# A recommender kernel on one core: the last group of rows weighed slot by slot, a gate with its constant folded in, and matrix products that nobody reads

## The chip, the core and the metric

The kernel runs on one core of a Trainium2 chip. The metric is the device time of one execution in microseconds (us); lower is better. Of the kernel before there are three timed runs (median 819.96 us) and one profiled execution.

## What is computed

2048 users and items, 100 history entries for each user; D is 128, the two layers have 1024 and 512 features. Cut to what matters:

```python
hist_emb = user_table[history_users]                       # 2048 x 100 rows of 128
scores = jnp.einsum('bhd,bd->bh', hist_emb, user_emb)
user_his_emb = jnp.einsum('bh,bhd->bd', scores, hist_emb)
x = jnp.concatenate([items_emb, user_his_emb, user_emb], axis=1)
x = _dice(_batchnorm(x @ W1 + b1, g1, be1), a1)            # statistics over the 2048 users
x = _dice(_batchnorm(x @ W2 + b2, g2, be2), a2)
return x @ W3 + b3

def _dice(x, alpha):
    avg = x.mean(axis=1, keepdims=True)
    var = jnp.sum((x - avg) ** 2 + DICE_EPS, axis=1, keepdims=True)
    ps = jax.nn.sigmoid((x - avg) / jnp.sqrt(var))
    return ps * x + (1.0 - ps) * alpha * x
```

## The kernel before, in words

Indices past the table's end count as its last row, so most history entries are the same row; the kernel sorts each user's keys, ranks the users by how many entries are that last row, and treats them in 16 tiles of 128 users. It has three stages.

**Gathering (to about 607 us).** For each tile, GpSimd gathers the history rows that are not the last one, 128 rows (one slot) to an indirect DMA (L406). Four slots are a group, four groups the ring `rows` (16 slots). `relay` waits for each slot of a group to land; only the fourth raises `arrived` (L413), on which VectorE waits. VectorE's `weigh` (L623 to L642) multiplies a group by the user's row (L628), sums (L633), masks (L637) and, with `feed`, hands the indices of a later group to GpSimd (L642). ScalarE scales the four slots by their scores (L879) and TensorE adds them into `pooled_ps` by products with the identity (`add_rows`, L1052). A tile's last group g1 is weighed after the loop over its groups (L675). Ahead of it VectorE takes the statistics of the tile before (`layer1_stats`, L621, 8 `bn_stats`). After it, in the last tile alone, it aggregates 15 tiles' statistics (L680, 8 `bn_aggr`), and TensorE makes the last part of the first layer (`layer1_pooled`, L1039, 8 products).

**First batch norm and gate, second layer (about 612 to 768 us).** VectorE makes scale and shift of the 1024 features (L684 to L708; ready at `bn_ready`). The 2048 users then go through in 9 chunks: 0 and 1 of 128 users, 2 to 8 of 256. Each engine has its own order, written out by hand in a function `step(i, live)`, in which `live(n)` holds the work for chunk i - n. A chunk goes through these pieces:

- normalise: ScalarE (L915), and for some feature blocks GpSimd (L441) or, for chunk 0, VectorE (L712)
- the average over features: for chunks 0 and 1 (`c < NARROW`) eight TensorE products with a matrix of 1/1024 (L1111); for the others VectorE adds eight blocks to one (L765, L771, L781) and TensorE makes one product (L1116)
- the deviation (VectorE L733), its square (ScalarE L933), sums (VectorE L758, L768, L776), the variance (TensorE L1123), root (ScalarE L927) and reciprocal (VectorE L741), spread to all lanes (TensorE L1137), times the deviation (VectorE L749), sigmoid (ScalarE L939)
- the mix: gate * (1 - alpha) + alpha, by VectorE for chunks 0 and 1 (L720), by GpSimd for the others (L448), then times x (VectorE L725, `dice_done`)
- the second layer: 32 products (TensorE L1093), 8 of them ahead of the next chunk's L1137 and 24 behind it; ScalarE adds the bias (L948)

Every engine works in its order and waits on semaphores, so TensorE's average of chunk c stands in its queue ahead of the products of chunk c - 2.

**Second batch norm, gate and output (768 us to the end).** TensorE turns the result (L1148), VectorE takes statistics, and for each tile a gate and a weighted sum follow (L1153, L831); GpSimd scatters the outputs (L457).

```python
def relay(q, count):                                    # L409, GpSimd
    for j in range(GROUP):
        pool.wait_ge(landed[q * GROUP + j], count)
        pool.sem_inc(arrived if j == GROUP - 1 else passed, 1)
```

## Time and profile before

| | before |
|---|---|
| median of three runs | 819.96 us (819.0 to 820.18) |
| the profiled execution, its own time | 820.12 us |
| its span in the trace | 818.0 us |
| mean granted clock of TensorE, as a share of 2.4 GHz | 0.87 |
| busy: TensorE 78%, VectorE 63%, GpSimd 61%, ScalarE 43% of the span | |

The trace names the engines PE (TensorE), PEld (its weight loads), DVE (VectorE), ACT (ScalarE) and POOL (GpSimd). A busy TensorE isn't one at full speed: the granted clock is 1.00 or 0.50 at any one time, which is 2.4 or 1.2 GHz, and a share between them in a stretch is a mixture. A product of 32-bit numbers appears as two matmul records, so 64 records of L1093 are 32 products. Where an engine is idle before an instruction, the row tells in square brackets for how long, and what ended it.

### The profile page before, as it was taken

The numbers are of one execution on the slowest core, as the hardware profiler recorded it, in microseconds if no ns is written. First come the engines' busy times: TensorE is split into PE (matmuls) and PEld (weight loads), VectorE is DVE, ScalarE is ACT, GpSimd is POOL, SyncE is SP. The second block draws the span as 40 slices with busy tenths as digits, with TensorE's granted clock in tenths as the row PEclk, the third lists the DMA queues.
The fourth block names the chain that finished last, engine by engine and source line by source line (L and its number), as shares of the span: only waits on it lengthen the run. The fifth ranks groups of instructions, "written<-read, shape, count | busy, mean of one in ns | idle before, by whom it ended". The sixth has DMA issues, their size and how long they took to land.

```text
span 818.0 us, 16371 instructions
## 1 busy us (share of the span) xinstructions
PE 640.0 (78%) x3374; PEld 534.2 (65%) x3374; DVE 518.4 (63%) x1422; ACT 351.7 (43%) x858; POOL 496.7 (61%) x519
## 2 busy tenths in 40 slices
PE   0475759787887879878878898798654889999794
PEld 0473648565766757666766686586544878888684
DVE  7933446656665656666756666675556879985383
ACT  0002325343442534434444445345437777663452
POOL 7772777776777777777777777777742045321025
PEclk9967968796988978789898989889686789999998
DMA  7980221221111212122221222222210000000000
GB/s 147 54 154 26 52 53 51 55 52 52 52 54 51 56 53 53 51 56 53 52 56 52 53 56 53 54 54 53 52 34 0 1 1 0 1 1 1 0 2 0
DMA packets 19640, 35.73 MB, mean 44 GB/s; under 512 B 10552, under 2 KB 10752, under 8 KB 19584
## 3 DMA queue, kind: packets, MB, share of 16 engines
q0 software_dynamic: 15360, 30.45, 17.7%
q1 hardware_dynamic: 4224, 4.59, 1.9%
q8 instruction: 28, 0.46, 0.2%
q14 instruction: 28, 0.23, 0.1%
HBM read 35.00 MB, written 0.01 MB: 43 GB/s over the span
## 4 chain that ended last, share of the span: by engine, by line
issue 30%; PE 28%; POOL 16%; DMA 12%; DVE 6%; ACT 3%; DVEq 2%; POOLq 1%; ACTq 1%; SPq 0%; PEldq 0%
PE ps L1093 13%; POOL rows L406 11%; DMA rows<-in_L_rec_user_table_dram,slot_idx 11%; PE ps L993 5%; PE ps L1052 3%; PE ps L984 2%; POOL wide L387 2%; PE ps L1153 2%; POOL wide L402 2%; ACT wide L959 1%; PE ps L1148 1%; DMA wide<-in_L_rec_item_table_dram,ids 1%; DVE prod L628 1%; PE ps L1039 1%; ACTq L320 1%
## 5 line engine op out<-in xcount | busy, mean ns | idle before, releaser
L406 POOL DMA_INDIRECT rows<-in_L_rec_user_table_dram,slot_idx x432 | 407.6, 944 | 149.7 <-issue 112.3
L879 ACT ACTIVATE scaled<-rows,work 128x128 f32 (+1 forms) x492 | 175.7, 400 | 195.2 <-DVE work L637 114.4
L1052 PE MATMUL ps<-ident,scaled 128*128 128x128 f32 x984 | 174.7, 323 | 95.1 <-ACT scaled L879 94.3
L1052 PEld LDWEIGHTS ps<-ident,scaled 128*128 128x128 f32 x984 | 152.8, 221 | 121.2 <-issue 112.6
L628 DVE TENSOR_TENSOR prod<-rows,ps 128x512 f32<-128x512 f32 x123 | 84.2, 684 | 121.3 <-POOLq L413 79.1
L993 PE MATMUL ps<-wide,h 128*128 128x360 f32 x448 | 156.2, 507 | 0.0
L993 PEld LDWEIGHTS ps<-wide,h 128*128 128x128 f32 x448 | 92.1, 211 | 51.7 <-issue 13.4
L1093 PE MATMUL ps<-h,w 128*128 128x256 f32 (+1 forms) x576 | 119.1, 368 | 1.3 <-DVE h L725 1.3
L1093 PEld LDWEIGHTS ps<-h,w 128*128 128x128 f32 x576 | 102.9, 199 | 13.1 <-DVE h L725 1.6
L633 DVE TENSOR_REDUCE work<-prod 128x512 f32 x123 | 84.3, 686 | 14.3 <-DVE prod L628 5.5
L448 POOL TENSOR_SCALAR work<-work,rest,alphas 128x2048 f32<-128x2048 f32 x7 | 20.1, 2877 | 91.6 <-ACT work L939 91.6
L529 DVE SCALAR_TENSOR_TENSOR h<-ps,col_no 128x1024 f32<-128x1024 f32 x28 | 34.3, 1224 | 54.0 <-ACT ranked L851 52.5
L1033 PE MATMUL ps<-both_T,w 128*128 128x128 f32 x512 | 63.8, 279 | 0.0
L1033 PEld LDWEIGHTS ps<-both_T,w 128*128 128x128 f32 x512 | 61.1, 196 | 0.0
L851 ACT ACTIVATE ranked<-ps 128x360 f32<-128x360 f32 x15 | 7.1, 470 | 106.7 <-PE ps L993 97.3
L1039 PE MATMUL ps<-pooled_T,w 128*128 128x128 f32 x256 | 47.9, 366 | 0.5 <-ACT pooled_T L902 0.5
L1039 PEld LDWEIGHTS ps<-pooled_T,w 128*128 128x128 f32 x256 | 46.7, 281 | 0.8 <-ACT pooled_T L902 0.8
L457 POOL DMA_INDIRECT out_dram<-y_col,perm x16 | 15.4, 964 | 46.2 <-DVE y_col L824 43.5
L637 DVE SCALAR_TENSOR_TENSOR work<-wide,ends_f,work x123 | 27.4, 223 | 22.9 <-issue 13.6
L984 PE MATMUL ps<-wide,h 128*128 128x128 f32 (+2 forms) x128 | 29.4, 416 | 15.3 <-DVE h L523 12.0
L984 PEld LDWEIGHTS ps<-wide,h 128*128 128x128 f32 x128 | 25.2, 281 | 19.1 <-DVE h L523 12.3
L871 ACT ACTIVATE h<-ps,par 128x128 f32<-128x128 f32 x128 | 35.9, 361 | 1.8 <-DVE stats L684 1.6
(173 smaller groups left out, 684.9 us busy)
## 6 DMA issues: line engine op xcount, KB each, us to landing
rows<-in_L_rec_user_table_dram,slot_idx POOLq DMA_INDIRECT x432, 2.5
w<-in_L_rec_W_dram SPq DMA_DIRECT2D x1, 2048.0 KB, 9.6
w<-in_L_rec_W_dram SPq DMA_DIRECT2D x1, 1536.0 KB, 9.6
h<-in_r_history_users_dram SPq DMA_DIRECT2D x1, 800.0 KB, 5.2
wide<-in_L_rec_user_table_dram,ids POOLq DMA_INDIRECT x16, 7.0
wide<-in_L_rec_item_table_dram,ids POOLq DMA_INDIRECT x16, 6.9
out_dram<-y_col,perm POOLq DMA_INDIRECT x16, 2.1
last_row<-in_L_rec_user_table_dram SPq DMA_DIRECT2D x1, 64.0 KB, 4.9
```

What stands on the lines that cost most here:

```text
L406: nc.gpsimd.indirect_dma_start(rows[:, s, :], None, user_table, bass.IndirectOffsetOnAxis(slot_idx[:, s:s + 1], 0)).then_inc(landed[s], 16)
L529: nc.vector.scalar_tensor_tensor(places[:, :, j, :], rank.rearrange("p (m j) -> p m j", j=2)[:, :, j].unsqueeze(2).to_broadcast(shape), -f ...
L628: nc.vector.tensor_tensor(prod[:, :, :], rows[:, at, :], user_now.unsqueeze(1).to_broadcast([P, GROUP, D]), ALU.mult).then_inc(multiplied, 1)
L633: nc.vector.tensor_reduce(raw[:, pair], prod[:, :, :], AX_X, ALU.add).then_inc(dotted, 1)
L871: nc.scalar.activation(h1[:, m, t * P:(t + 1) * P], l1_ps[:, m, :], ACT.Identity, bias=b1c[:, m:m + 1]).then_inc(l1_kept, 1)
L879: nc.scalar.activation(scaled[:, j, :], rows[:, bass.ds((g & (GROUPS - 1)) * GROUP + j, 1), :], ACT.Copy, scale=score[:, bass.ds(g * GROUP ...
L984: mm = nc.tensor.matmul(place_ps, at_place[:, t, :], people[:, t, x], start=(t == 0), stop=(t == TILES - 1))
L993: mm = nc.tensor.matmul(rows_ps[(t + 1) % 2], places[:, m, j, :], people[:, 2 * m + j, :], start=(j == 0 and m == 0), stop=(j == 1 and m = ...
L1033: nc.tensor.matmul(l1_ps[:, m, :], w1[:, k, m * P:(m + 1) * P], both_T[:, of:of + P], start=(k == 0 and m == blocks.start), stop=False, sk ...
L1039: mm = nc.tensor.matmul(l1_ps[:, m, :], w1[:, 1, m * P:(m + 1) * P], pooled_T[:, :], start=False, stop=True, skip_group_check=True)
L1052: nc.tensor.matmul(pooled_ps, scaled[:, j, :], ident[:, :], start=False, stop=False, skip_group_check=True).then_inc(slot_summed, 1)
L1093: mm = nc.tensor.matmul(l2_ps[c % 2][:, o, 0:w], w2[:, k, o * P:(o + 1) * P], h1[:, k, chunk(c)], start=(k == 0), stop=(k == M1 - 1))
```

## The change

- `relay` raises `arrived` for each slot; `weigh` waits for `g * 4 + 4`. The last group of the last tile is weighed by a new `weigh_end`, slot by slot, and ScalarE scales each slot on its own score (`end_scored`).
- In the last tile the loop over groups is split after four of them; between the two parts stand `layer1_stats` of the tile before and the 8 `bn_aggr`, which stood ahead of and behind the last group.
- The mix is gone on both engines. The gate adds alpha / (1 - alpha) (`over`) in the multiplication by x, and the factor 1 - alpha (`rest`) is the scale of the second layer's bias step on ScalarE.
- `DIRECT = 4`: chunks 0 to 3 have their averages by eight TensorE products; VectorE's adding begins with chunk 4.
- `keep_busy` issues products of the identity with itself into a bank that is written anew before anything reads it: 8 ahead of the last group's `add_rows`, 12 after the last `layer1_pooled`, 5 after chunk 0's variance and 10 after chunk 0's L1137.

```diff
@@ relay (GpSimd)
-                    pool.sem_inc(arrived if j == GROUP - 1 else passed, 1)
+                    pool.sem_inc(arrived, 1)
@@ step (GpSimd)
-                if live(2) and i - 2 >= NARROW:
-                    c = i - 2
-                    pool.wait_ge(gated, c + 1)
-                    nc.gpsimd.tensor_scalar(dev_of(c), dev_of(c), rest[:, 0:1], alphas[:, 0:1],
-                                            ALU.mult, ALU.add).then_inc(mixed, 1)
                 if live(-1):
                     normalise(i + 1)
@@ weigh and weigh_end (VectorE)
-                hold(dve, arrived, g + 1)
+                hold(dve, arrived, g * GROUP + GROUP)
...
+            def weigh_end(g, t, bound):
+
+                for j in range(GROUP):
+                    hold(dve, arrived, g * GROUP + (j + 1))
+                    one = bass.ds(g * GROUP + (t * GROUP + j), 1)
+                    nc.vector.tensor_tensor(prod[:, j:j + 1, :], rows[:, bass.ds((g & (GROUPS - 1)) * GROUP + j, 1), :],
+                                            user_now.unsqueeze(1), ALU.mult).then_inc(end_multiplied, 1)
+                    dve.wait_ge(end_multiplied, j + 1)
+                    nc.vector.tensor_reduce(raw[:, one], prod[:, j:j + 1, :], AX_X, ALU.add).then_inc(end_dotted, 1)
+                    dve.wait_ge(end_dotted, j + 1)
+                    nc.vector.scalar_tensor_tensor(score[:, one], slot_no[:, bass.ds(g * GROUP + j, 1)], bound, raw[:, one],
+                                                   ALU.is_lt, ALU.mult).then_inc(end_scored, 1)
@@ the loop over tiles (VectorE)
-                with dve.Fori(0, g1 - g0) as r:
+                with dve.Fori(0, g1 - g0 if t + 1 < TILES else GROUPS) as r:
...
+                if t + 1 == TILES:
+
+                    layer1_stats(t - 1)
+                    dve.wait_ge(stats_done, M1 * t)
+                    for m in range(M1):
+                        nc.vector.bn_aggr(mv[:, m, :], stats1[:, m, 0:t, :].rearrange("p t s -> p (t s)")).then_inc(bn_step[0], 1)
+                    with dve.Fori(GROUPS, g1 - g0) as r:
+                        g = dve.snap(r + g0).with_bounds(max_val=HIST * (t + 1) // GROUP - 1)
+                        weigh(g, t, ALU.is_ge, ends_f[:, t:t + 1], True)
...
-                if t:
+                if t and t + 1 < TILES:
                     layer1_stats(t - 1)
-                weigh(g1, t, ALU.is_lt, ends_f[:, t + 1:t + 2])
-
-
-            dve.wait_ge(stats_done, M1 * (TILES - 1))
-            for m in range(M1):
-                nc.vector.bn_aggr(mv[:, m, :], stats1[:, m, 0:TILES - 1, :].rearrange("p t s -> p (t s)")).then_inc(bn_step[0], 1)
+                if t < TILES - 1:
+                    weigh(g1, t, ALU.is_lt, ends_f[:, t + 1:t + 2])
+                else:
+                    weigh_end(g1, t, ends_f[:, t + 1:t + 2])
@@ step (VectorE)
-                    if c < NARROW:
-                        dve.wait_ge(gated, c + 1)
-                        nc.vector.tensor_scalar(dev_of(c), dev_of(c), rest[:, 0:1], alphas[:, 0:1],
-                                                ALU.mult, ALU.add).then_inc(mixed_first, 1)
-                        dve.wait_ge(mixed_first, c + 1)
-                    else:
-                        dve.wait_ge(mixed, c - NARROW + 1)
-                    nc.vector.tensor_tensor(h1[:, :, chunk(c)], by_block(dev_of(c), M1), h1[:, :, chunk(c)],
-                                            ALU.mult).then_inc(dice_done, 1)
+                    dve.wait_ge(gated, c + 1)
...
+                    nc.vector.scalar_tensor_tensor(h1[:, :, chunk(c)], by_block(dev_of(c), M1), over[:, 0:1], h1[:, :, chunk(c)],
+                                                   ALU.add, ALU.mult).then_inc(dice_done, 1)
...
-                if live(0) and i >= NARROW:
+                if live(0) and i >= DIRECT:
@@ scale_rows and step (ScalarE)
+                by_slot = t == TILES - 1 and after is end_scaled
+                if not by_slot:
+                    hold(act, scored, g + (t + 1))
                 for j in range(GROUP):
+                    if by_slot:
+                        act.wait_ge(end_scored, j + 1)
...
                         nc.scalar.activation(h2[:, k, chunk(c)], l2_ps[c % 2][:, k, 0:w], ACT.Identity,
-                                             bias=b2c[:, k:k + 1]).then_inc(l2_kept, 1)
+                                             bias=b2c[:, k:k + 1], scale=rest[:, 0:1]).then_inc(l2_kept, 1)
@@ TensorE
+            def keep_busy(count):
+
+                for _ in range(count):
+                    nc.tensor.matmul(idle_ps, ident[:, :], ident[:, :], start=True, stop=True)
...
+                if t == TILES - 1:
+                    keep_busy(8)
                 add_rows(g1, t, True)
...
             layer1_pooled(TILES - 1)
+            keep_busy(12)
...
-                    if c < NARROW:
+                    if c < DIRECT:
```

TensorE's order from the end of the first layer to the first products of the second, before (`mean_of` is the matrix of 1/1024, `h` the features, `w` the weights):

```order
L1039 MATMUL ps<-pooled_T,w 128x128 x8
L1111 MATMUL ps<-h,mean_of 128x128 x16
L1123 MATMUL ps<-ones,sq_sum 128x1
L1137 MATMUL ps<-ident,inv 128x128
L1116 MATMUL ps<-col_sum,mean_of 128x256
L1123 MATMUL ps<-ones,sq_sum 128x1
L1093 MATMUL ps<-h,w 128x128 x8
```

and with the change:

```order
L1066 MATMUL ps<-pooled_T,w 128x128 x8
L1049 MATMUL ps<-ident 128x128 x12
L1141 MATMUL ps<-h,mean_of 128x128 x16
L1153 MATMUL ps<-ones,sq_sum 128x1
L1049 MATMUL ps<-ident 128x128 x5
L1169 MATMUL ps<-ident,inv 128x128
L1049 MATMUL ps<-ident 128x128 x10
L1141 MATMUL ps<-h,mean_of 128x256 x8
L1153 MATMUL ps<-ones,sq_sum 128x1
L1123 MATMUL ps<-h,w 128x128 x8
```

The unread products are the rows `ps<-ident`; chunk 2's average, one product of 256 columns, is eight and still stands ahead of chunk 1's variance and of the products of chunk 0.

VectorE's order from chunk 0's L749 to its multiplication by x, before:

```order
L749 TENSOR_TENSOR work<-work,ps 128x1024
L758 TENSOR_TENSOR rows<-rows 128x512
L765 TENSOR_TENSOR w<-h 128x1024
L768 TENSOR_TENSOR rows<-rows 128x256
L771 TENSOR_TENSOR w<-w 128x512
L776 TENSOR_TENSOR sq_sum<-rows 128x128
L781 TENSOR_TENSOR col_sum<-w 128x256
L720 TENSOR_SCALAR work<-work,rest,alphas 128x1024
L725 TENSOR_TENSOR h<-work,h 128x8x128
L733 TENSOR_TENSOR work<-h,ps 128x2048
```

and with the change (`over` is alpha / (1 - alpha)):

```order
L767 TENSOR_TENSOR work<-work,ps 128x1024
L776 TENSOR_TENSOR rows<-rows 128x512
L786 TENSOR_TENSOR rows<-rows 128x256
L794 TENSOR_TENSOR sq_sum<-rows 128x128
L743 SCALAR_TENSOR_TENSOR h<-work,over,h 128x8x128
L751 TENSOR_TENSOR work<-h,ps 128x2048
```

Four instructions are gone from between the two: three of chunk 2's adding and the mix; the multiplication is one instruction with three inputs.

VectorE's order in the last tile, from the end of the loop over groups to the aggregation, before:

```order
L667 COMPARE_AND_BRANCH
L621 BN_STATS stats<-h 128x6 x8
L313 ISA
L628 REGISTER_ALU
L628 ISA
L628 TENSOR_TENSOR prod<-rows,ps 128x512
L313 REGISTER_ALU
L633 ISA
L633 TENSOR_REDUCE work<-prod 128x4
L637 ISA
L637 SCALAR_TENSOR_TENSOR work<-wide,ends_f,work 128x4
L680 BN_AGGR mv<-stats 128x2 x8
```

and with the change, from the end of the loop's first part:

```order
L679 COMPARE_AND_BRANCH
L620 BN_STATS stats<-h 128x6 x8
L688 BN_AGGR mv<-stats 128x2 x8
L689 UNCONDITIONAL_BRANCH
L689 ISA
L627 REGISTER_ALU
L627 ISA
L627 TENSOR_TENSOR prod<-rows,ps 128x512
```

Both statistics now stand ahead of the loop's second part, in which (at L627) a whole group is still weighed; the last group's slots follow after that. On GpSimd the 16 normalisations, which stood in pairs behind the mixes from the ninth on, follow each other, with nothing to wait for after the scale and shift.

## Rows read from the trace of the kernel before

**Rows 1.** The page: busy time, share of the span and instructions by engine.

```profile
PE 640.0 (78%) x3374; PEld 534.2 (65%) x3374; DVE 518.4 (63%) x1422; ACT 351.7 (43%) x858; POOL 496.7 (61%) x519
```

**Rows 2.** By stretches: length, busy of PE, PEld, DVE, ACT, POOL; granted clock; DMA.

```profile
606.90:612.30 5.40, 2.05 (x8) 1.78 (x8) 4.85 (x11) 1.48 (x5) 0.00 (x0) 0.65 0.00 0
620.00:624.10 4.10, 3.89 (x18) 3.92 (x19) 1.12 (x6) 3.15 (x9) 3.96 (x8) 0.50 0.00 0
630.60:637.00 6.40, 1.44 (x5) 1.21 (x5) 6.37 (x10) 6.29 (x9) 0.00 (x0) 0.50 0.00 0
657.10:662.10 5.00, 1.85 (x7) 1.62 (x7) 5.00 (x5) 4.39 (x10) 5.00 (x2) 0.76 0.00 0
662.10:668.20 6.10, 6.10 (x20) 5.05 (x21) 2.20 (x2) 3.20 (x3) 0.73 (x2) 0.64 0.00 1
668.20:768.30 100.10, 99.67 (x483) 87.99 (x481) 73.01 (x80) 53.15 (x75) 27.83 (x12) 1.00 0.00 1
```

**Rows 3.** GpSimd's four releases of the last group (one line's instructions, 601.5 to 607).

```profile
L413 POOLq EVENT_SEMAPHORE  x4: 17/17/17, 601.9 to 606.5; - x4
```

**Rows 4.** The timeline, last tile: start us, us, engine, line [idle before].

```profile
595.86 0.69 DVE L628 TENSOR_TENSOR prod<-rows,ps 128x512 f32<-128x512 f32 x1 [1.19 <-POOLq L413]
...
600.87 0.69 DVE L628 TENSOR_TENSOR prod<-rows,ps 128x512 f32<-128x512 f32 x1 [2.75 <-POOLq L413]
...
603.69 1.65 DVE L621 BATCH_NORM_STATS2 stats<-h 128x6 f32<-128x128 f32 x8 [0.57 <-issue]
...
606.88 0.69 DVE L628 TENSOR_TENSOR prod<-rows,ps 128x512 f32<-128x512 f32 x1 [1.54 <-POOLq L413]
...
608.80 0.22 DVE L637 SCALAR_TENSOR_TENSOR work<-wide,ends_f,work  x1 [0.29 <-DVE work L633]
...
608.94 3.49 DVE L680 BATCH_NORM_AGGREGATE mv<-stats 128x2 f32<-128x90 f32 x8
...
612.60 3.35 PE L1039 MATMUL ps<-pooled_T,w 128*128 128x128 f32 x16 [0.46 <-ACT pooled_T L902]
```

**Rows 5.** The timeline from the first scale and shift to the first product of L1093.

```profile
619.65 4.32 POOL L441 TENSOR_SCALAR h<-h,scale,shift 128x128 f32<-128x128 f32 x8 [15.67 <-DVE shift L708]
...
619.65 1.37 DVE L712 TENSOR_SCALAR h<-h,scale,shift 128x128 f32<-128x128 f32 x5
...
620.21 6.37 PE L1111 MATMUL ps<-h,mean_of 128*128 128x128 f32 x32 [4.26 <-ACT h L915]
...
624.00 1.22 DVE L733 TENSOR_TENSOR work<-h,ps 128x1024 f32<-128x1024 f32 x1 [2.98 <-PE ps L1111]
...
629.66 0.80 PE L1137 MATMUL ps<-ident,inv 128*128 128x128 f32 x2 [1.40 <-DVE inv L741]
...
630.50 1.22 DVE L749 TENSOR_TENSOR work<-work,ps 128x1024 f32<-128x1024 f32 x1 [0.89 <-PE ps L1137]
...
632.24 1.22 DVE L765 TENSOR_TENSOR w<-h 128x1024 f32<-128x1024 f32 x1
...
634.85 0.80 DVE L720 TENSOR_SCALAR work<-work,rest,alphas 128x1024 f32<-128x1024 f32 x1
...
635.68 1.23 DVE L725 TENSOR_TENSOR h<-work,h 128x1024 f32<-128x1024 f32 x1
...
636.97 3.79 PE L1093 MATMUL ps<-h,w 128*128 128x128 f32 x16 [0.48 <-DVE h L725]
```

**Rows 6.** The timeline of chunk 2, from its L749 to its products.

```profile
651.50 5.52 PE L1093 MATMUL ps<-h,w 128*128 128x128 f32 x48
...
651.70 2.29 DVE L749 TENSOR_TENSOR work<-work,ps 128x2048 f32<-128x2048 f32 x1 [0.87 <-PE ps L1137]
...
656.09 3.13 POOL L448 TENSOR_SCALAR work<-work,rest,alphas 128x2048 f32<-128x2048 f32 x1 [32.13 <-ACT work L939]
...
657.38 2.11 DVE L776 TENSOR_TENSOR sq_sum<-rows 128x256 f32<-128x256 f32 x1
...
659.75 2.28 DVE L725 TENSOR_TENSOR h<-work,h 128x2048 f32<-128x2048 f32 x1
...
662.08 5.91 PE L1093 MATMUL ps<-h,w 128*128 128x256 f32 x16 [0.28 <-DVE h L725]
...
668.28 10.53 PE L1093 MATMUL ps<-h,w 128*128 128x256 f32 x48
```

**Rows 7.** Groups of instructions by form: count, busy us, mean ns, idle before.

```profile
L529 DVE SCALAR_TENSOR_TENSOR h<-ps,col_no 128x1024 f32<-128x1024 f32 x28 | 34.3, 1224 | 54.0 <-ACT ranked L851 52.5 <-issue 0.2
...
L653 DVE COPY ps<-ranked 128x128 f32<-128x128 f32 x16 | 4.7, 295 | 9.2 <-DVE work L637 9.2
```

46 lines of the change are left out of this document (27 added, 19 removed).

## The prediction

> **What bounds the kernel now.** I read the page first. TensorE is the busiest engine at 78% [rows 1], but a share of the whole span hides three stages with three limits, so I went on to the busy times by stretches, and then to the timeline around the places that the diff touches. Up to 607 us the gathers on GpSimd set the pace. From 668.20 to 768.30 TensorE is busy for 99.67 of 100.10 us at clock 1.00 [rows 2]: there nothing helps but fewer products. The last 50 us (818.0 - 768.3) aren't touched by the diff, except for where two constants are kept. What is left is the stretch of 61 us between 607 and 668, in which TensorE waits for others, falls to half its clock and then works at half: the granted clock is 0.65 in 606.90:612.30, 0.50 in 620.00:624.10, 0.50 in 630.60:637.00, and 0.64 in 662.10:668.20, where it is busy all the time [rows 2]. A gain can come from there alone, and it counts only as far as chunk 2's products (L1093 at 662.08 [rows 6]) start earlier or run faster, since from there on TensorE has no gap.
>
> **The last group and the statistics.** Two edits meet here. The statistics were 8 `bn_stats` of 1.65 us and 8 `bn_aggr` of 3.49 us [rows 4]. The `bn_aggr` cost nothing where they were: they ended at 612.43 (608.94 + 3.49), and L1039, on which VectorE's next work depends, began only at 612.60 [rows 4]. So moving them gains nothing by itself; it is needed only if the last group gets shorter. The last tile has five groups in its loop, the fourth at 595.86 and the fifth at 600.87 [rows 4]; the new place is behind the fourth. A group takes 2.26 us (600.87 to its end at 603.12, which is where the idle 0.57 us before L621 began). So the fourth ends at 598.12, and behind it come 0.57 us of loop end, 5.14 us of statistics and some 0.3 us of loop start: the fifth group starts at 604.1 in place of 600.87 and ends at 606.4. The slots of the last group are released from 601.9 to 606.5 [rows 3], so when VectorE comes to them at about 607.1 all four are there, and going slot by slot no longer hides any of their landing. It now costs: a slot is three instructions, two of about 0.29 us (128x128, the copy L653 [rows 7]) and one of 0.22 (L637 [rows 4]), with some 0.15 us between dependent ones (0.26 to 0.29 before, where two register waits stand between), about 1.15 us in all. The fourth score is there at 607.1 + 4 x 1.15 = 611.7, where all four were at 609.02 (L637 [rows 4]). In return ScalarE and TensorE have one slot left to do, not four: from the score to L1039 it was 3.58 us (612.60 - 609.02), and is about 1.8. L1039 starts at 613.5, so **0.9 us later**. Of TensorE: the fifth group's additions end at 608.9, then come the 8 unread products, at half clock 8 x 0.42 = 3.4 us (L1039 has 8 in 3.35 us [rows 4]), so until 612.3; the slots' additions go behind them, and are just not held up. TensorE is then busy from 607.5 on without a long gap. L1111 tells how its clock comes back: 16 products in 6.37 us [rows 5], where all at half would be 6.7 and all at full 3.8, and 0.50 until 624.10 [rows 2]; so it rose some 5 us after the work began. L1039 should then run at the full clock: 8 x 0.24 = 1.9 us in place of 3.35 (24 products of 128 columns take 5.52 us, L1093 at 651.50 [rows 6]), **1.4 us less**. Together the scale and shift come 0.3 us earlier, since VectorE's own statistics of the last tile then pace it. Ends: 1.2 us later (no full clock), 1.8 us earlier (VectorE needs 0.95 us a slot and less for the loop's ends).
>
> **The first two averages.** The 12 unread products take 2.9 us at full clock in a gap of 4.26 us (idle before L1111 [rows 5]). If they keep the clock up, chunk 0's average ends 1.2 us after VectorE's last normalisation (L712 ends at 621.0 [rows 5], then 620.7; the rest of it are the last products and the way to VectorE), and L733, at 624.00 [rows 5], comes at about 622.4, allowing 0.5 us for ScalarE's share. **1.6 us earlier**, the 0.3 from above in it. From here to L749 the chain is one of dependent steps that don't change, ScalarE's normalisation of chunk 2 among them: L749 at 628.8 for 630.50.
>
> **Chunk 0's gate and its products.** Behind L749 VectorE loses four instructions: L765, L771 and L781, of 1024, 512 and 256 columns, and the mix L720. From L765 to L725 it was 3.44 us (632.24 to 635.68 [rows 5]), in which only two small sums stay, 0.7 us together by their size against L765's 1.22 for 1024 columns; 2.7 us go. The multiplication stays as long: with three inputs 128x1024 takes 1224 ns at L529 [rows 7], with two 1.23 us at L725 [rows 5]. So L725 could start at 631.3 for 635.68. But TensorE isn't ready. Ahead of the products it has 10 unread ones (2.4 us) and chunk 2's average, which was one product and is eight of 0.44 us (24 in 10.53 us, L1093 [rows 6]), 3.5 us. L1137 began at 629.66 and took 0.80 us at half clock [rows 5]; 1.7 us earlier and at full it ends at 628.5, and 628.5 + 2.4 + 3.5 and 0.1 for a variance gives 634.5, or **2.5 us earlier** than 636.97 [rows 5], and the 10 unread products are a part of what holds it up.
>
> **Chunk 2, where it counts.** From 634.5 at full clock: 32 products of 0.24 us with L1137 between them, and a wait of 0.7 us for it, until about 643.0, then chunk 3's average in 3.6 us, until 646.6; chunk 3's deviation starts at 646.8 and chunk 2's L749 at 649.9, for 651.70 [rows 6]: **1.8 us earlier**. Of the 2.5 us and of the half clock in chunk 0's products most goes into two averages that are each 7 x 0.44 = 3.1 us longer. From L749 to L725 it was 8.05 us (651.70 to 659.75 [rows 6]). There the mix of GpSimd shows: L776 takes 2.11 us for 256 columns, while L448 runs beside it [rows 6]; without it 256 columns should take 0.4 (512 take 0.69, L628 [rows 4]). The mix is gone, so **1.6 us** go too. L725 starts at 656.3, chunk 2's products at 658.7. Then the clock: before, 0.64 over 6.10 us is 4.4 us at half, which cost 2.2 us. TensorE's idle time ahead was 3.1 us (it worked 1.85 of 5.00 in 657.10:662.10 [rows 2]) and is about the same now, so it may fall or not; I take half, **1.0 us**.
>
> **GpSimd's normalisations** take 0.54 us each (8 in 4.32 us, L441 [rows 5]); 16 now run in one go, from 619.3 to 628. In the trace nothing on VectorE that reads two tiles of SBUF stood beside the first eight. The Trainium skill (SBUF — State Buffer, Who interferes with whom) says that a VectorE instruction with two SBUF inputs and a GpSimd instruction that reads SBUF exclude each other, whole instruction by whole instruction; L776 beside L448 agrees, with 2.11 us. By that rule L758, L768 and L776 of chunk 0, at 625 to 627, can each wait 0.54 us, up to 1.6 us, and the sum below would be 817.2. From the rows alone the bounds are 0 (L441 beside L712 showed no delay) and 3 x 0.54 = 1.6; I take 0, as TensorE, not this chain, holds up chunk 0's products, and keep 1.6 for the range.
>
> **Other edits** are worth nothing: one register instruction more in VectorE's wait for a group lies under gathers that VectorE waits for (idle 2.75 and 1.54 us before L628 [rows 4]), and the scale 1 - alpha is in an instruction that is there anyway.
>
> **The sum.** 1.8 (of which 0.3 and 1.3 come from the first two parts) + 1.6 + 1.0 = 4.4 us. The profiled execution had 820.12 us, 2.1 over its span and 0.16 over the median; 819.96 - 4.4 = 815.6 us. A measurement of this kernel tells 0.2%, 1.6 us, from no change.
>
> **The rivals.**
> - *The clock holds.* The clock stays full from the last group to the end: then chunk 2's 2.2 us come back whole, and with the last group at its better end (1.5 us) the time is 815.6 - 1.2 - 1.5 = 812.9. The Trainium skill (TensorE: Matmul & The Clock Gate, What's actually happening) says that the half clock is the default and activity lifts it; for it speaks 668 to 768 at 1.00, against it that a gap of 3 us stays ahead of chunk 2. Chance 0.20.
> - *Late and in the way.* VectorE's chain is later by the last group (1.2) and by the normalisations (1.6), and this passes on to chunk 2; what stays is 4.4 - 2.8 = 1.6, and without the 1.0 of the clock 0.6: 819.4. Chance 0.12.
> - *Unread products at half clock.* They do not lift the clock, and stand in TensorE's order. The last group and L1039: 1.2 us later. The 12 take 5.0 us in a gap of 4.26: 0.8. The 5 take 2.1 us where at most 1.4 us were idle (before L1137 [rows 5]): 0.7. Then 10 take 4.2 us, and chunk 2's average at half 7.0: chunk 0's products start at 630.46 + 2.7 + 4.2 + 7.1 = 644.5, 7.5 us late. From there TensorE is no longer waiting, and what it lost before (1.9 us at half clock in the first eight of chunk 0's products, 3.79 for 1.9 [rows 5], half as much in the rest, 3.1 idle, 2.2 in chunk 2's) is 8.1 us, against 3.1 for chunk 3's average: 7.5 + 3.1 - 8.1 = 2.5 us slower, 822.5. It decides if the granted clock is still 0.50 while chunk 2's average runs. For it: 0.50 over all of 630.60:637.00 [rows 2] and little real work there; against: at 620.21 the clock did rise under products of the same size. Chance 0.08.
>
> **How the numbers follow.** The forecast has 0.60, from 813 to 818.3 by its own bounds (the last group 1.5 to either side, the clock 1.1, the normalisations 1.6). Its slower edge reaches into no change only a little. Faster by over 0.2%: 0.60 + 0.20 = 0.80. Within: 0.12. Slower: 0.08. The range is 811.8 to 819.2 us, which leaves out the third rival, some of the second and the far end of the first.
>
> **What would show it.** Right: the fifth group's L628 near 604 and the last score near 611.7; L1039's eight products in 2 us, not 3.35; L733 of chunk 0 at 622.4, its products at 634.5 at clock 1.00; sums of squares for chunk 2 in 0.4 us; chunk 2's products at 658.7; the stretch from there to the end as before. Wrong: a granted clock of 0.50 under the unread products before chunk 2's average, a chunk 0 whose L758 to L776 are stretched, or products of chunk 2 that start no earlier than 661.

## The result and the profile after

| | before | after |
|---|---|---|
| median of the runs | 820.05 us (8 runs, 819.0 to 820.97) | 812.27 us (8 runs, 809.95 to 816.31) |
| ratio, 95% interval | | 0.9908, 0.9889 to 0.9926 |
| profiled execution, its span | 820.12, 818.0 us | 812.3, 810.5 us |
| granted clock of TensorE, mean | 0.87 | 0.889 |

The kernel became 7.8 us faster where 4.4 were forecast. That is inside the range, 0.5 us from its faster end, and next to the rival "the clock holds" (812.9). The page of the changed kernel, busy times, against [rows 1]: GpSimd lost seven instructions and 30 us, VectorE 11 us, and neither number says where the gain is.

```profile
PE 637.8 (79%) x3472; PEld 533.6 (66%) x3472; DVE 507.3 (63%) x1423; ACT 355.3 (44%) x858; POOL 466.9 (58%) x512
```

The changed kernel by stretches (the columns are those of [rows 2]):

```profile
606.50:611.83 5.33, 4.87 (x28) 4.63 (x28) 2.24 (x9) 1.92 (x6) 0.00 (x0) 0.68 0.01 3
617.60:621.70 4.10, 3.54 (x29) 3.46 (x30) 2.59 (x6) 3.49 (x9) 4.10 (x8) 1.00 0.00 0
626.50:632.30 5.80, 5.80 (x40) 5.39 (x38) 3.83 (x5) 5.77 (x9) 0.32 (x1) 1.00 0.01 3
651.14:656.14 5.00, 2.57 (x21) 2.28 (x20) 5.00 (x7) 4.98 (x12) 0.00 (x0) 1.00 0.00 0
656.14:662.34 6.20, 6.20 (x31) 5.53 (x32) 4.21 (x3) 4.62 (x4) 0.00 (x0) 1.00 0.00 1
662.34:759.73 97.39, 97.39 (x471) 85.94 (x469) 64.54 (x80) 55.50 (x73) 0.00 (x0) 1.00 0.00 1
```

The three places that were at 0.50, 0.50 and 0.64 are at 1.00: the first average, the wait for chunk 0's gate, chunk 2's products. The long stretch is as full as before.

The last tile of the changed kernel, from the timeline (fifth group, slots, unread products, first layer's end; answers to [rows 4]):

```profile
597.26 1.65 DVE L620 BATCH_NORM_STATS2 stats<-h 128x6 f32<-128x128 f32 x8
598.94 3.50 DVE L688 BATCH_NORM_AGGREGATE mv<-stats 128x2 f32<-128x90 f32 x8
602.36 0.63 DVE L627 TENSOR_TENSOR prod<-rows,ps 128x512 f32<-128x512 f32 x1
...
605.11 0.29 DVE L648 TENSOR_TENSOR prod<-rows,ps 128x128 f32<-128x128 f32 x1 [0.59 <-issue]
...
606.35 0.29 DVE L648 TENSOR_TENSOR prod<-rows,ps 128x128 f32<-128x128 f32 x1
...
607.15 3.33 PE L1049 MATMUL ps<-ident 128*128 128x128 f32 x16
...
609.74 0.22 DVE L653 SCALAR_TENSOR_TENSOR work<-wide,ends_f,work  x1 [0.18 <-DVE work L651]
...
611.83 2.05 PE L1066 MATMUL ps<-pooled_T,w 128*128 128x128 f32 x16 [0.46 <-ACT pooled_T L924]
```

The slots come 1.24 us apart, the last score is there at 609.96, and the first layer's last products take 2.05 us for 3.35. From the first scale and shift to chunk 2's products (answers to [rows 5] and [rows 6]):

```profile
617.59 9.23 POOL L445 TENSOR_SCALAR h<-h,scale,shift 128x128 f32<-128x128 f32 x16 [14.62 <-DVE shift L729]
...
618.15 4.07 PE L1141 MATMUL ps<-h,mean_of 128*128 128x128 f32 x32 [1.59 <-ACT h L937]
620.48 1.22 DVE L751 TENSOR_TENSOR work<-h,ps 128x1024 f32<-128x1024 f32 x1 [1.51 <-PE ps L1141]
...
622.69 3.04 ACT L937 ACTIVATE h<-h,shift,scale 128x256 f32<-128x256 f32 x6
...
623.56 0.66 DVE L786 TENSOR_TENSOR rows<-rows 128x256 f32<-128x256 f32 x1
624.25 0.53 DVE L794 TENSOR_TENSOR sq_sum<-rows 128x128 f32<-128x128 f32 x1
...
625.64 0.24 ACT L949 ACTIVATE root<-ps,var_eps 128x1 f32<-128x1 f32 x1
...
628.74 3.62 PE L1141 MATMUL ps<-h,mean_of 128*128 128x256 f32 x16
629.47 1.28 DVE L743 SCALAR_TENSOR_TENSOR h<-work,over,h 128x1024 f32<-128x1024 f32 x1 [0.15 <-ACT work L961]
632.33 2.03 PE L1123 MATMUL ps<-h,w 128*128 128x128 f32 x16
...
647.38 2.29 DVE L767 TENSOR_TENSOR work<-work,ps 128x2048 f32<-128x2048 f32 x1 [0.87 <-PE ps L1169]
...
653.06 0.42 DVE L794 TENSOR_TENSOR sq_sum<-rows 128x256 f32<-128x256 f32 x1
653.73 2.35 DVE L743 SCALAR_TENSOR_TENSOR h<-work,over,h 128x2048 f32<-128x2048 f32 x1
653.96 0.67 PE L1146 MATMUL ps<-col_sum,mean_of 128*128 128x256 f32 x2 [1.26 <-DVE col_sum L799]
...
656.14 3.71 PE L1123 MATMUL ps<-h,w 128*128 128x256 f32 x16 [1.17 <-DVE h L743]
```

Chunk 2's products start at 656.14 for 662.08 [rows 6], and its first eight take 3.71 us for 5.91.

**Where the 7.5 us of span came from.** Each line is the difference between two neighbouring points in the two traces (R is the release of the last slot, 606.5 before and 605.7 after; S is the end of VectorE's last instruction for the shift, L708 before and L729 after, 0.1 us ahead of GpSimd's first normalisation).

| stretch | before | after | difference |
|---|---|---|---|
| start to R | 606.5 | 605.7 | -0.8 |
| R to the first layer's last products | 6.10 | 6.13 | 0.0 |
| from there to S | 6.95 | 5.66 | -1.3 |
| S to chunk 0's deviation | 4.45 | 2.99 | -1.5 |
| to chunk 0's multiplication by the reciprocal | 6.50 | 6.23 | -0.3 |
| to chunk 0's products | 6.47 | 5.62 | -0.9 |
| to chunk 2's multiplication by the reciprocal | 14.73 | 15.05 | +0.3 |
| to chunk 2's multiplication by x | 8.05 | 6.35 | -1.7 |
| to chunk 2's products | 2.33 | 2.41 | +0.1 |
| to the end of the second layer's products | 105.79 | 103.59 | -2.2 |
| to the end of the span | 50.13 | 50.77 | +0.6 |

In a second profile of the change (after2, below) R is at 604.6 and the first layer's last products start 6.7 us after it, not 6.1; all other lines are the same to 0.03 us.

### The profile page after: what moved, and what is told of

It is laid out like the page before. It is cut to its first block, busy times and chain, and to the rows that moved or that the text cites. A ratio compares the mean times of both kernels' runs of the same rounds, so it can differ in the third digit from the quotient of the medians.

```text
span 810.5 us, 16579 instructions
## 1 busy us (share of the span) xinstructions
PE 637.8 (79%) x3472; PEld 533.6 (66%) x3472; DVE 507.3 (63%) x1423; ACT 355.3 (44%) x858; POOL 466.9 (58%) x512
## 4 chain that ended last, share of the span: by engine, by line
PE 31%; issue 27%; POOL 15%; DMA 13%; DVE 6%; ACT 2%; DVEq 2%; ACTq 1%; POOLq 1%; SPq 0%; PEldq 0%
PE ps L1123 13%; DMA rows<-in_L_rec_user_table_dram,slot_idx 12%; POOL rows L410 11%; PE ps L1015 6%; PE ps L1079 3%; PE ps L1182 2%; POOL wide L391 2%; PE ps L1006 2%; PE ps L1187 2%; POOL wide L406 2%; PE ps L1141 1%; DVE prod L627 1%; DMA wide<-in_L_rec_item_table_dram,ids 1%; ACT scaled L901 1%; ACTq L324 1%
## 5 line engine op out<-in xcount | busy, mean ns | idle before, releaser
L627 DVE TENSOR_TENSOR prod<-rows,ps 128x512 f32<-128x512 f32 x122 | 83.5, 684 | 119.5 <-POOLq L417 94.8
L1015 PEld LDWEIGHTS ps<-wide,h 128*128 128x128 f32 x448 | 92.2, 212 | 51.4 <-issue 12.5
L1123 PE MATMUL ps<-h,w 128*128 128x256 f32 (+1 forms) x576 | 114.3, 357 | 1.2 <-DVE h L743 1.2
L1123 PEld LDWEIGHTS ps<-h,w 128*128 128x128 f32 x576 | 98.8, 190 | 12.2 <-DVE h L743 1.2
L1060 PE MATMUL ps<-both_T,w 128*128 128x128 f32 x512 | 65.7, 284 | 0.0
L1060 PEld LDWEIGHTS ps<-both_T,w 128*128 128x128 f32 x512 | 62.8, 200 | 0.0
L1066 PE MATMUL ps<-pooled_T,w 128*128 128x128 f32 x256 | 41.1, 329 | 0.5 <-ACT pooled_T L924 0.5
L1066 PEld LDWEIGHTS ps<-pooled_T,w 128*128 128x128 f32 x256 | 40.1, 246 | 0.6 <-ACT pooled_T L924 0.6
L1006 PE MATMUL ps<-wide,h 128*128 128x128 f32 (+2 forms) x128 | 26.7, 387 | 17.3 <-DVE h L522 12.0
L1006 PEld LDWEIGHTS ps<-wide,h 128*128 128x128 f32 x128 | 22.5, 252 | 21.1 <-DVE h L522 12.3
L561 DVE MAX8 top<-ranked 128x8 f32<-128x104 f32 x108 | 28.3, 262 | 3.2 <-issue 1.8
```

Of the source, the lines that this page charges most:

```text
L627: nc.vector.tensor_tensor(prod[:, :, :], rows[:, at, :], user_now.unsqueeze(1).to_broadcast([P, GROUP, D]), ALU.mult).then_inc(multiplied, 1)
L1006: mm = nc.tensor.matmul(place_ps, at_place[:, t, :], people[:, t, x], start=(t == 0), stop=(t == TILES - 1))
L1015: mm = nc.tensor.matmul(rows_ps[(t + 1) % 2], places[:, m, j, :], people[:, 2 * m + j, :], start=(j == 0 and m == 0), stop=(j == 1 and m = ...
L1060: nc.tensor.matmul(l1_ps[:, m, :], w1[:, k, m * P:(m + 1) * P], both_T[:, of:of + P], start=(k == 0 and m == blocks.start), stop=False, sk ...
L1066: mm = nc.tensor.matmul(l1_ps[:, m, :], w1[:, 1, m * P:(m + 1) * P], pooled_T[:, :], start=False, stop=True, skip_group_check=True)
L1123: mm = nc.tensor.matmul(l2_ps[c % 2][:, o, 0:w], w2[:, k, o * P:(o + 1) * P], h1[:, k, chunk(c)], start=(k == 0), stop=(k == M1 - 1))
```

## The experiments

Twelve runs were made: ten new kernels, the change once more, and one of the ten twice. Two readings are compared. One is the time, as a ratio to the kernel before on the same chip. The other is taken from each profile: **A**, from the start of the first layer's last products to chunk 2's first products, and **B**, from there to the end of the second layer's products. A is what the waits are worth, B says whether the clock held under chunk 2's products (103.6: held; 105.8: as before). "To S" is the first part of A, up to the shift. Each A and B is of one profile.

| kernel | to S | A | B | A+B | ratio, 95% interval |
|---|---|---|---|---|---|
| before | 6.95 | 49.48 | 105.79 | 155.27 | |
| the change | 5.66 | 44.31 | 103.59 | 147.90 | 0.9908 (0.9889 to 0.9926) |
| after2, the change again | 5.64 | 44.30 | 103.58 | 147.88 | 0.9925 (0.9909 to 0.994) |
| b_fold, folded gate alone | 6.96 | 45.96 | 103.58 | 149.54 | 0.9923 (0.9909 to 0.9937) |
| b_kb, unread products alone | 6.84 | 47.13 | 105.16 | 152.29 | 0.9965 (0.9954 to 0.9977) |
| b_direct *, DIRECT = 4 alone | 5.65 | 48.06 | 105.77 | 153.83 | 0.9999 (0.9986 to 1.0011) |
| b_end *, last group and statistics alone | 7.01 | 49.55 | 105.82 | 155.37 | 1.0063 (1.0039 to 1.0088) |
| a_nokb *, the change without unread products | 7.00 | 46.67 | 103.60 | 150.27 | 1.0025 (1.0005 to 1.0045) |
| a_nofold *, the change with the mix | 5.65 | 47.06 | 105.49 | 152.55 | 1.0026 (1.0008 to 1.0045) |
| a_direct2 *, the change with DIRECT = 2 | 5.65 | 42.10 | 105.27 | 147.37 | 0.9979 (0.9962 to 0.9996) |
| a_aggr_behind2, aggregations behind the slots | 5.84 | 44.49 | 103.58 | 148.07 | 0.9903 (0.9884 to 0.9922) |
| a_aggr_behind *, the same kernel | 5.85 | 46.06 | 103.59 | 149.65 | 0.9977 (0.9956 to 0.9999) |
| aggr_d2 *, that with DIRECT = 2 | 5.84 | 43.63 | 105.05 | 148.68 | 0.996 (0.9938 to 0.9981) |
| aggr_d2_no10 *, and without the 10 unread products | 5.83 | 45.08 | 103.59 | 148.67 | 0.9968 (0.9952 to 0.9983) |

The rows marked * come from two occasions on which every kernel took some 240 to 256 us more: the kernel before 1075.87 and 1059.47 us, and their ratios are to these. The gathering stage is longer there (in the list of waits ScalarE's scaling of slots has 199 to 282 us in these eight profiles put down to "remote", which is none of this core's engines, and nothing in the others), and the cause stays open. A and B begin behind it and can be compared, but with care for the part to S: which clock TensorE has there comes out of the gathering, and b_direct, whose last group is the old one, has a full clock there where the kernel before has half. The ratios there hold, too, what happens at the end of a gathering in which ScalarE is behind, and a last stage that is 2 to 5 us longer. So the times that were expected for these kernels can't be compared with those measured. The change itself wasn't run on these occasions. How much of its gain is left there isn't known: a_direct2, whose A+B is 7.9 us under that of the kernel before, was 0.2% faster there, and a_nokb, with 5.0 us less, 0.25% slower.

**One part taken out of the change.** Unread products (`keep_busy(0)` at the four places), then DIRECT, then the mix (GpSimd for chunks from 2, VectorE for 0 and 1):

```diff
-                    keep_busy(8)
+                    keep_busy(0)
...
-    DIRECT = 4
+    DIRECT = 2
...
-                    nc.vector.scalar_tensor_tensor(h1[:, :, chunk(c)], by_block(dev_of(c), M1), over[:, 0:1], h1[:, :, chunk(c)],
-                                                   ALU.add, ALU.mult).then_inc(dice_done, 1)
...
+                        dve.wait_ge(mixed, c - NARROW + 1)
+                    nc.vector.tensor_tensor(h1[:, :, chunk(c)], by_block(dev_of(c), M1), h1[:, :, chunk(c)],
+                                            ALU.mult).then_inc(dice_done, 1)
```

> The changed kernel without any of the 35 unread products; all else as changed. Theory A (the clock is what the unread products buy, and it made the part of the gain that the forecast lacked): the granted clock is 0.50 again under the first layer's last products and under chunk 0's average, L733's successor comes 2 us later, chunk 0's products partly run at 0.50, and the time is 815 to 816.5. Theory B (the unread products fill waits that others bridge, and partly stand in the way: 10 of them and chunk 2's average lie ahead of chunk 0's products): what the clock loses is won back by products that start earlier, time 811.5 to 813.

Measured: A grows by 2.36 us, B not at all. The first layer's last products take 3.40 us again and S comes 7.00 us after their start (5.66 with them), chunk 0's deviation 4.16 us after S (2.99). Behind that nothing is lost: chunk 0's products run at full clock, and the clock under chunk 2's products holds without unread products. This is nearer theory A (2.4 us, where it had 2.7 to 4.2 over the change), but without its third part, products of chunk 0 at 0.50. The part to S (1.3 us) can't be put down to the unread products with certainty: b_kb has them and its first layer's last products are at half clock (3.25 us), b_direct has none and its are at full (2.05).

> The changed kernel with the averages of chunks 2 and 3 made by VectorE's sums again (DIRECT = 2). Theory A (TensorE is the one that is waited for here, as the forecast has it: each of the two averages costs it 7 x 0.44 = 3.1 us): chunk 2's products start 1 to 2 us earlier, time 810.5 to 811.5. Theory B (VectorE's chain sets chunk 2, and 2.1 us of sums for each of two chunks come back onto it, and TensorE gets a gap that costs its clock): 813.5 to 815.

Measured: A is 2.2 us shorter and B 1.7 longer. The averages by products do cost TensorE time ahead of chunk 2, as theory A had it, and 1.7 of the 2.2 us are given back by the clock, which fell. Chunk 2's products in this kernel, in the columns of [rows 2]:

```profile
911.14:917.34 6.20, 6.20 (x23) 5.23 (x24) 2.53 (x3) 4.62 (x4) 0.00 (x0) 0.72 0.00 1
```

> The changed kernel with the mix gate * (1 - alpha) + alpha back as instructions of its own, on VectorE for chunks 0 and 1 and on GpSimd for the others. Theory A (the mix cost through the wait that it gave VectorE's sum of squares, 1.7 us on chunk 2's path, and 0.8 us on VectorE for chunks 0 and 1 that TensorE's queue hides): that sum takes 2.1 us again for chunk 2, time 814 to 815. Theory B (all of the mix is on the path, 0.8 + 0.8 + 2.9 us, and the longer gap costs the clock under chunk 2's products too, 2.2 us): 816.5 to 819. Theory C (the mix was hidden): 812 to 813.

Measured: A is 2.75 us longer and B 1.9. The sum of squares of chunk 2 takes 2.11 us again, and the clock under chunk 2's products falls again (0.69 over 6.2 us). At 4.65 us in all this is theory B, with the clock in it.

**The folded gate alone, the unread products alone, the change again.** b_fold and b_kb are the kernel before with one part; both keep `arrived` per slot, a register instruction more for each group, and the last tile's loop in two parts, as b_direct below does.

> The changed kernel itself, unchanged, beside the other three of its group, since the first four experiments ran where the kernel before takes 1075.9 us and not 820 (ScalarE waits 282 us there in the gathering). Theory A (the difference of the two kernels lies behind the gathering and comes again wherever it runs): 6 to 9 us under the kernel before, TensorE's stretch from the first layer's last products to the second layer's end 147 to 149 us. Theory B (part of it was the gathering's own spread, 1.1 us in the first pair of traces): 4 to 6 us under it.

> The kernel before with the folded gate alone (no unread products, averages of chunks 2 and up by VectorE, last group and statistics in their old order). Theory A (its price is the 1.7 us that VectorE's sum of squares waited for the mix of chunk 2, and on chunks 0 and 1 the 0.8 us of the mix, which here nothing of TensorE's hides): 2.5 to 3.5 us under the kernel before. Theory B (VectorE and TensorE alternate, so a shorter wait of TensorE also keeps its clock under chunk 2's products, 2.2 us more): 4.5 to 6 us under it. Theory C: under 1 us.

> The kernel before with the 35 unread products alone. Theory A (the clock's share): chunk 0's deviation 2 to 3 us earlier and chunk 0's products at full clock (2.8 us less), but chunk 1's gate is VectorE's to make, so of it 3 to 4.5 us remain at the end. Theory B (without the earlier gate the 10 unread products stand in nobody's way, but chunk 2's products wait for VectorE as before and the clock falls ahead of them as before): 1 to 2.5 us.

Measured: the change repeats to 0.02 us in A+B, and to 0.6 us in time. **The folded gate alone gives 6.6 us** (812.70 for 819.33), which six runs of each don't tell from the change measured beside it (6.5), the unread products alone 3.2 (816.17). By A+B it is 5.7 of 7.4; b_fold's profiled execution is the longest of its six (814.96). So the fold is most of the change, and its clock under chunk 2's products held: that is theory B, in time a little over its range. b_kb has the size of its theory A, but not all of its mechanism: chunk 0's deviation is 1.6 us earlier (1.5 of it behind S), and the clock fell to 0.50 soon after the start of chunk 0's products. The timeline of b_fold and of b_kb at chunk 2's products:

```profile
658.86 3.70 PE L1122 MATMUL ps<-h,w 128*128 128x256 f32 x16 [1.18 <-DVE h L742]
```

```profile
659.23 5.28 PE L1132 MATMUL ps<-h,w 128*128 128x256 f32 x16 [1.10 <-DVE h L752]
```

With 35 unread products and the mix most of the clock's fall stays; with neither there is none. What the fold does there is seen in the two groups of the sums of squares for 256 users, in the kernel before and in the change:

```profile
L776 DVE TENSOR_TENSOR sq_sum<-rows 128x256 f32<-128x256 f32 x7 | 11.4, 1626 | 0.0
```

```profile
L794 DVE TENSOR_TENSOR sq_sum<-rows 128x256 f32<-128x256 f32 x7 | 2.9, 421 | 0.1
```

1626 ns for 421 on average: with the mix beside them they were held up (single ones took 2.11 us, those without a mix beside them 0.42), and behind each, in VectorE's order, stands the last addition for a later chunk's average (L781 before, L799 now), for which TensorE waits. The wait ahead of chunk 4's average, which stands right ahead of chunk 2's products, is 1.26 us in the change (L1146 above). In the kernel before it was more than twice that (the wait behind it is longer now, 1.17 us for 0.28):

```profile
659.97 1.19 PE L1116 MATMUL ps<-col_sum,mean_of 128*128 128x256 f32 x2 [2.95 <-DVE col_sum L781]
```

**The two other parts alone**, on the kernel before (`DIRECT` as above; for b_end the slots, and the statistics inside the last tile's loop):

> The kernel before with one part alone: averages by eight TensorE products for chunks 2 and 3. It takes four or more instructions' worth of VectorE time (2.1 us by its rows, beside chunk 0's gate) and adds 2 x 3.1 us at full clock to TensorE, 2 x 6.2 at half. Theory A (TensorE has that time to spare before chunk 2): chunk 2's products start within 1 us of 662.1, time 819 to 821. Theory B (it stands in the way of chunk 0's and chunk 1's products): chunk 2's products start 3 us or more later, time 822 to 824.

> The kernel before with one part alone: the last group slot by slot, with the statistics and the aggregations inside the last tile, no unread products. By the changed kernel's trace the slots come 4.3 to 4.5 us after the last release and the first layer's last products 6.1 to 6.8 us after it, for 6.1 in the kernel before, so this part alone gives nothing. Theory A: first layer's last products 6.1 to 6.8 us after the last release, at half clock, time 819.5 to 821. Theory B (the slots' pitch is hidden): they start 4 to 5 us after the last release, time 817.5 to 818.5.

Measured: b_direct's A is 1.4 us shorter, but 1.3 of that lie ahead of S, where the averages play no part: its first layer's last products met a full clock, which its part, acting later, can't have caused. From S to chunk 2's products it is 42.4 us for 42.5, so DIRECT = 4 alone gives 0.1 us, and the time is the same within 0.14%. That is theory A. The eight products for chunk 2 began at half clock and took 6.3 us, as theory B feared; but behind them chunk 0's first products ran at full clock, 2.03 us for 3.79:

```profile
851.15 2.05 PE L1075 MATMUL ps<-pooled_T,w 128*128 128x128 f32 x16 [0.46 <-ACT pooled_T L933]
...
867.51 6.29 PE L1150 MATMUL ps<-h,mean_of 128*128 128x256 f32 x16
...
873.78 2.03 PE L1132 MATMUL ps<-h,w 128*128 128x128 f32 x16
```

b_end's A is unchanged, but its time is 7 us **longer**, outside both expectations. Its timeline, last tile:

```profile
840.80 1.65 DVE L627 BATCH_NORM_STATS2 stats<-h 128x6 f32<-128x128 f32 x8 [9.52 <-ACT h L899]
842.48 3.50 DVE L695 BATCH_NORM_AGGREGATE mv<-stats 128x2 f32<-128x90 f32 x8
845.90 0.63 DVE L634 TENSOR_TENSOR prod<-rows,ps 128x512 f32<-128x512 f32 x1
```

The statistics wait for ScalarE's copy of the tile before (VectorE is idle for 9.52 us), and the fifth group, which doesn't need them, stands behind. b_direct, with the old order, waits for the same copy, but with the last group alone behind it:

```profile
834.94 0.69 DVE L634 TENSOR_TENSOR prod<-rows,ps 128x512 f32<-128x512 f32 x1 [3.00 <-issue]
...
841.82 1.65 DVE L627 BATCH_NORM_STATS2 stats<-h 128x6 f32<-128x128 f32 x8 [4.65 <-ACT h L898]
843.39 0.67 DVE L634 TENSOR_TENSOR prod<-rows,ps 128x512 f32<-128x512 f32 x1
```

The last slots were released alike, at 840.1 and 840.5. In b_direct the last score comes at 845.49, in b_end at 853.50: 3.5 us later by the aggregations, 2.7 by the fifth group (845.90 to 848.65), 2.8 because four slots one by one take 4.85 us where a group takes 2.1, less the 1.0 us by which the copy was earlier. aggr_d2, with the `bn_stats` alone inside, lies between (840.7, 850.58). In the 812 us profiles ScalarE is on time and L620 waits for nothing; there the slots one by one and the old group came out alike, since the first layer's last products start 6.1 to 6.7 us after the release where it was 6.1.

**The aggregations behind the slots**, an edit that keeps the rest of the change:

```diff
@@ the loop over tiles, if t + 1 == TILES
                     layer1_stats(t - 1)
-                    dve.wait_ge(stats_done, M1 * t)
-                    for m in range(M1):
-                        nc.vector.bn_aggr(mv[:, m, :], stats1[:, m, 0:t, :].rearrange("p t s -> p (t s)")).then_inc(bn_step[0], 1)
@@ behind the last group
                     weigh_end(g1, t, ends_f[:, t + 1:t + 2])
+                    dve.wait_ge(stats_done, M1 * t)
+                    for m in range(M1):
+                        nc.vector.bn_aggr(mv[:, m, :], stats1[:, m, 0:t, :].rearrange("p t s -> p (t s)")).then_inc(bn_step[0], 1)
```

> The changed kernel with the 8 aggregations (3.5 us) moved out of the last tile's loop to behind the last group's slots; the 8 statistics of the tile before stay between the loop's parts. Theory A (the aggregations made the fifth group 2.6 us late, and slot by slot lost its use as all four slots had landed): the fifth group is weighed as soon as it has landed, the last score comes some 3 us earlier relative to the last landing, the first layer's last products 2.5 to 3 us earlier, time 809 to 810.5. Theory B (TensorE's 8 unread products at half clock hold the last additions anyway): the additions start where they did relative to the fifth group's, 0.5 to 1.5 us gained at most, time 811 to 812.

> The kernel of a_aggr_behind again (the 8 aggregations behind the last group's slots), where the gathering sets the pace. There it was ahead of the changed kernel's other variants by 1.5 to 6 us, but the last group had landed 10 us before it was weighed. Theory A: the last score 1.5 to 2.5 us after the last slot's release (4.3 in the changed kernel, 2.5 before), the first layer's last products 2 to 3 us earlier, 2 to 3 us under the changed kernel. Theory B (the 8 unread products run at half clock, 3.3 us, behind the fifth group's additions, and hold the last ones): 0.5 to 1.5 us under it.

Measured: 810.87 us median (809.28 to 812.61), ratio 0.9903. The last score is 2.07 us after the last release (4.26 and 4.49 in the two profiles of the change), and from that release to the end of the span it is 202.8 us, for 204.8 and 205.5. That is theory A. Against the change the gain of 2 to 3 us is seen in the traces (a_aggr_behind on the other occasion has the first layer's last products 12.3 us after the release, the three kernels with the aggregations inside 15.5 to 15.9); the times of the two, 810.87 and 812.87 (after2), have ratios whose intervals overlap. The `bn_stats` stayed inside the tile here; with them behind as well it wasn't tried.

The same kernel's A differs by 1.6 us between its two profiles. The timelines, first of the long condition, then of the other, around chunk 0's variance:

```profile
878.80 0.59 PE L1153 MATMUL ps<-ones,sq_sum 128*128 128x1 f32 x2 [2.61 <-DVE sq_sum L794]
...
879.25 2.48 PE L1049 MATMUL ps<-ident 128*128 128x128 f32 x10
...
882.20 1.22 DVE L767 TENSOR_TENSOR work<-work,ps 128x1024 f32<-128x1024 f32 x1 [2.15 <-PE ps L1169]
```

```profile
623.33 0.38 PE L1153 MATMUL ps<-ones,sq_sum 128*128 128x1 f32 x2 [2.62 <-DVE sq_sum L794]
...
623.57 1.36 PE L1049 MATMUL ps<-ident 128*128 128x128 f32 x10
...
625.19 1.22 DVE L767 TENSOR_TENSOR work<-work,ps 128x1024 f32<-128x1024 f32 x1 [0.63 <-PE ps L1169]
```

After the same wait of 2.6 us the clock is at half in one and full in the other. At half the five unread products take 2.48 us, stand ahead of L1169, and VectorE waits 2.15 us where it otherwise waits 0.63. This is the third rival in small: where unread products don't find a full clock, they are in the way.

**DIRECT = 2 and no ten unread products on top:**

> The changed kernel with two edits: the eight aggregations behind the last group's slots again, and the averages by eight products for chunks 0 and 1 only (VectorE adds from chunk 2 on). Theory A, the four products-averages are nearly free since their time on TensorE lies in front of chunk 2, where TensorE waits for VectorE anyway: the stretch from the first layer's last products to the end of the second layer's takes 147.4 to 148 us as with the aggregations alone (148.07), time 810.5. Theory B, they are what the sum of the parts is short by (6.6 from the folded gate and 3.2 from the unread products give 9.8, the whole change only 7): the stretch takes 145 us or less, and the time is 807.8.

> The same kernel without the ten unread products behind chunk 0's spread reciprocal; the 8, 12 and 5 stay. Theory A, they only stand in the way, as chunk 2's clock holds without them (it did with the folded gate alone): chunk 0's products start up to 2.4 us earlier, and the end of the second layer's products is the same or up to 1 us earlier, since VectorE's chain to chunk 2 sets it. Theory B, they hold the clock over the wait for chunk 0's gate: without them the granted clock is 0.50 under chunk 0's products again and the stretch is 1 to 2 us longer, time 811.5 to 812.5.

Measured: aggr_d2 has A 43.63 and B 105.05, so again earlier and at a fallen clock; A+B is 148.68, 0.7 us over the upper end of theory A, and far from B's 145. Without the ten, A+B is the same, 148.67. It has the 1.5 us of five slow unread products in it (VectorE waits 2.19 us there), and in return the clock held under chunk 2's products. Its two theories aren't told apart by that, since the two effects came together. But in both kernels, with the ten and without, the granted clock is 0.50 under chunk 0's first products (0.50 and 0.51 over their first 4 us), so here the ten didn't hold it.

**Why the parts don't add.** Taken from S to the end of the second layer's products, the parts alone give 5.7 us (fold), 2.9 (unread), 0.2 (DIRECT) and 0.0 (last group): 8.8, where the change gives 6.1. The kernel with three of them, a_direct2, gives 6.6. Up to chunk 2's products the three do add (6.1 us, for 5.8 as single parts); behind that they don't (0.5 for 2.8), because the clock fell there, which it didn't with the fold alone. DIRECT = 4 on top takes 2.2 us back ahead of chunk 2's products and gives 1.7 behind it. The change's other 1.3 us lie ahead of S, where the first layer's last products are at full clock; of the parts alone only b_direct has them, and its part acts behind S.

## Why the prediction was right, and where its sizes were off

**The sum.** 4.4 us were forecast, and the span lost 7.5. From the last slot's release on, against the forecast's own steps: about 1.0 us more up to the scale and shift, 0.2 in the first averages, 0.2 up to chunk 0's multiplication by the reciprocal, 0.4 from chunk 0's products to chunk 2's, 1.2 by the clock, and 0.6 less in the last stage. The other 0.8 us is the last slot's release, earlier in this one profile (605.7; after2 had 604.6, b_fold 606.8, before 606.5), which no part of the change explains.

**The last group.** The mechanism was mostly as forecast: the fifth group is held up by the statistics, VectorE then waits for no slot (it comes to the first at 605.11, and the last is released at 605.7), their pitch is 1.24 us (1.15 forecast), and the step from the last score to L1066 is 1.87 (1.8). But the step "L1039 starts at 613.5, so 0.9 us later" came out at 0.0 against the last release, and at 0.7 in after2. The term for 0.57 us of loop end and 0.3 of loop start was too large: from the fourth group's start (594.90) to the statistics it is 2.36 us, not 2.83, and the fifth group starts 0.1 us before the eight aggregations of 3.50 end. The full clock gave 1.3 us (1.4 forecast). S came 1.3 us earlier against the last release, and 0.7 in after2, where 0.3 was taken. What lifted the clock here is shown only in part: all eight profiles with both the slots one by one and the unread products have the first layer's last products in 2.05 us, one of these two alone isn't enough (3.25 in b_kb, 3.41 in b_end), and b_direct has 2.05 with neither.

**The first two averages.** 1.5 us (1.3 forecast behind S): the twelve unread products keep the clock, and b_kb shows it alone (2.99 us from S to the deviation, for 4.45). b_direct is the other side of it: a full clock under the first layer's last products, none of the twelve behind them, and 4.5 us.

**Chunk 0's gate and products.** L743 ended at 630.75 and the products began at 632.33, behind chunk 2's eight-product average, as forecast. The step from L767 to the products was 5.62 us for a forecast 5.7.

**Chunk 2.** From its L767 to its multiplication by x 1.7 us went (1.6 forecast), the sum of squares in 0.42 us. The size was right, the reason only in part: the multiplication also needed the mix itself, which ended at 659.22 (656.09 + 3.13 [rows 6]), 0.5 us before it began. So by these rows an unstretched sum beside the mix would have given an estimated 0.5 us; the other 1.2 came from having no mix to wait for.

**The clock under chunk 2's products is the term that was mis-sized**: "it may fall or not; I take half, 1.0 us". It held, and 2.2 us came back. The reason given for the half, that TensorE's idle time ahead "is about the same now", was wrong: it worked 2.57 of the 5 us, for 1.83 before (the same stretch ahead of the products), because the mix had also held up the average of chunk 4. But the idle time alone doesn't decide, since a_direct2 has the same 2.57 and fell to 0.72. So the half was a fair guess on what the rows told; the rival had the better number, and the better mechanism.

**GpSimd's normalisations.** They were taken as 0, and cost 0, though they did stretch the sums: L776, L786 and L794 of chunk 0 take 0.70, 0.66 and 0.53 us beside L445, where chunk 1's, without it, take 0.68, 0.43 and 0.29 (in the kernel before, where GpSimd had already ended, chunk 0's take 0.69, 0.43 and 0.29). That is 0.5 us of the 1.6 allowed, and in a_nokb, where the first one takes 1.15, 0.9. It lies under ScalarE's normalisations of chunk 2 (L937 above), behind which the root stands: from chunk 0's deviation to the root it is 5.16 us in the change, 5.17 before and 5.17 in b_kb, whose sums aren't stretched. So the 0 was right, by another reason than the one given. The rule of the Trainium skill (SBUF — State Buffer, Who interferes with whom) is seen here with 0.02 to 0.5 us for each instruction, less than a whole GpSimd instruction of 0.58 us; with the mix it was 1.2 us on average and 1.7 for chunk 2's (2.11 us for 0.42), of an instruction of 3.13 us.

**The last stage**, forecast unchanged, gave back 0.6 us. Behind the second layer TensorE waits for the statistics; then the clock is 0.50 where it was 0.71. The first row is of the kernel before, the second of the change, both from 5 us after the end of the second layer's products:

```profile
772.87:777.87 5.00, 4.93 (x32) 4.86 (x32) 3.58 (x10) 5.00 (x8) 0.00 (x0) 0.71 0.00 0
```

```profile
764.73:769.73 5.00, 4.84 (x23) 4.87 (x24) 3.34 (x8) 5.00 (x8) 0.00 (x0) 0.50 0.00 0
```

**The rivals.** "The clock holds" is what happened: in both profiles of the change the granted clock is 1.00 from ahead of the first layer's last products to the end of the second layer's (610.1 to 763 in the first). It had a chance of 0.20; that its number and the forecast's both lie in the range says little for the forecast's half. "Late and in the way" found only the 0.5 us of stretched sums, which cost nothing. "Unread products at half clock" didn't happen in the change's two profiles, but in two of other kernels, where it cost 1.5 us. One sum was off on paper: the forecast's own bounds give 819.8 on the slower side (815.6 + 1.5 + 1.1 + 1.6), not 818.3; nothing measured hangs on it. The change's first eight runs spread over 6 us, its second six over 2; no profile shows what the slower ones had.
